# Routed experts in two parts of the tokens (six pairs of images and two), with the first part's expert blocks starting before the last pair is routed

## The reference

```python
x = x + conv_ref(group_norm(x))      # filters of 7x7 made per image from softmax keys, layer norm, relu;
                                     # then a depthwise 7x7 convolution with them
t = to_tokens(x)                     # (16, 256, 128)
t = t + attention(layer_norm(t))     # tanh features, softmax(q q^T / sqrt(128)) times the tokens, per image
# mixture of experts on layer_norm(t), 4096 tokens, 8 experts, hidden size 256, the best 2 of 8 per token:
scores = xf @ router_w + router_b
topk_p, topk_i = top_k(softmax(scores), 2)
h = xf @ w1[e] + b1[e]
gated = silu(h @ wg[e] + bg[e]) * (h @ wv[e] + bv[e])
y = gated @ w2[e] + b2[e]
t = t + sum over the 2 chosen experts of topk_p * y
```

## Time and profile before

| | |
|---|---|
| profiled execution, its own time | 386.41 us |
| its span, first to last instruction | 384.6 us |
| median of 3 runs | 386.43 us |
| busy share of the span | PE 79%, DVE 62%, POOL 43%, ACT 34% |
| first multiplication of a block | at 243.86 us |
| last scatter issued | at 360.52 us |
| granted TensorE clock, mean | 0.87 of full speed |

### The profile page before, as it was taken

The page is one execution under the profiler, slowest core; times in us unless marked ns, Lnnn a source line. Parts: engine busy times, 40 slices in busy tenths (PEclk is TensorE's granted clock), DMA queues, the critical chain, the costliest instruction groups (busy, mean ns, idle before and its releaser), DMA issues.

```text
span 384.6 us, 7449 instructions
## 1 busy us (share of the span) xinstructions
PE 302.8 (79%) x1731; PEld 239.7 (62%) x1732; DVE 236.7 (62%) x1006; ACT 132.4 (34%) x443; POOL 164.2 (43%) x187
## 2 busy tenths in 40 slices
PE   1686989998989899998876661599999999999200
PEld 1264667786868777777664440388878787888100
DVE  2433475488887877676866652266666676666164
ACT  0312221425152515141303012266656565666000
POOL 3000010030256565555455577046656566666400
PEclk9958896999999999989887655599999999999755
DMA  7722241221523000101010013223332322231197
GB/s 221 250 80 67 84 125 28 85 68 30 182 79 97 31 30 21 38 21 37 22 35 29 29 56 107 55 80 81 85 94 84 89 77 83 80 93 59 48 322 288
DMA packets 29945, 33.37 MB, mean 87 GB/s; under 512 B 5096, under 2 KB 23740, under 8 KB 29658
## 3 DMA queue, kind: packets, MB, share of 16 engines
q1 hardware_dynamic: 23312, 22.00, 18.9%
q0 software_dynamic: 4384, 8.60, 6.7%
q10 hardware_dynamic: 2218, 2.42, 1.8%
HBM read 21.76 MB, written 11.75 MB: 87 GB/s over the span
## 4 chain that ended last, share of the span: by engine, by line
PE 44%; issue 21%; POOL 21%; DMA 5%; DVE 4%; SPq 3%; ACT 1%; POOLq 0%; DVEq 0%; ACTq 0%
POOL rows_dram L410 15%; PE bank L1324 8%; PE bank L1312 5%; PE bank L1307 5%; PE bank L1308 5%; PE bank L1317 4%; PE bank L833 3%; DMA w_high<-moe_dram 2%; PE bank L876 2%; POOL ln_rstd L437 2%; PE bank L1302 2%; SPq L1160 2%; PE bank L978 2%; POOL ln_rstd L433 2%; PE bank L914 1%
## 5 line engine op out<-in xcount | busy, mean ns | idle before, releaser
L1132 POOL DMA_INDIRECT moe_dram<-ys,xs x72 | 70.4, 978 | 51.2 <-issue 30.8
L410 POOL DMA_INDIRECT rows_dram<-row,slot x64 | 62.7, 979 | 18.2 <-issue 18.2
L1324 PE MATMUL bank<-w_all,gatedt 128*128 x288 | 44.1, 276 | 0.2 <-ACT gatedt L1175 0.2
L1249 DVE SCALAR_TENSOR_TENSOR ys<-b_all,xs,bank 128x128 f32<-128x128 f32 x72 | 25.0, 347 | 28.5 <-issue 27.0
L1259 DVE SCALAR_TENSOR_TENSOR gated<-bank,xs,silu 128x256 f32<-128x256 f32 x72 | 34.8, 483 | 10.2 <-ACT silu L1183 7.8
L1183 ACT ACTIVATE silu<-bank 128x256 f32<-128x256 f32 x72 | 27.6, 383 | 35.7 <-PE bank L1312 35.7
L1324 PEld LDWEIGHTS bank<-w_all,gatedt 128*128 128x128 f32 x288 | 38.0, 192 | 0.4 <-issue 0.4
L1307 PE MATMUL bank<-w_high,x_high 128*128 x72 | 35.6, 494 | 0.0
L978 PE MATMUL bank<-zhat,const 121*128 121x256 f32 (+1 forms) x128 | 31.2, 399 | 0.0
L1312 PE MATMUL bank<-w_high,x_low 128*128 x72 | 30.3, 421 | 0.7 <-issue 0.7
L423 POOL TENSOR_TENSOR frstd<-fvar,minus_half 128x2 f32<-128x2 f32 x8 | 5.7, 708 | 57.5 <-DVE fvar L703 57.5
(11 more groups left out here) (172 smaller groups left out, 593.7 us busy)
## 6 DMA issues: line engine op xcount, KB each, us to landing
xs<-rows_dram SPq DMA_DIRECT2D x72, 66.0 KB, 1.8
xc<-in_x SPq DMA_DIRECT2D x8, 256.0 KB, 2.9
wgv<-in_wg SPq DMA_DIRECT2D x8, 256.0 KB, 2.9
wgv<-in_wv SPq DMA_DIRECT2D x8, 256.0 KB, 3.4
xt<-in_xt SPq DMA_DIRECT2D x4, 512.0 KB, 4.6
xt<-moe_dram SPq DMA_DIRECT2D x8, 256.0 KB, 6.0
w_high<-moe_dram SPq DMA_DIRECT2D x8, 256.0 KB, 6.6
out<-w_high ACTq DMA_DIRECT2D x8, 256.0 KB, 5.6
```

Source lines behind the costliest of these rows:

```text
L410: pool.indirect_dma_start(rows_dram, bass.IndirectOffsetOnAxis(ap=slot[:, f % 2, 2 * t + k:2 * t + k + 1], axis=0), row[:, f % 2, t, k, :] ...
L1132: pool.indirect_dma_start(moe_dram, bass.IndirectOffsetOnAxis(ap=xs[:, u, C + 1:C + 2].bitcast(U32), axis=0), ys[:, u, :], None, bounds_ch ...
L1324: last = pe.matmul(bank_y[v][:, 0:C], gatedt[:, v, h * P:(h + 1) * P], w2_all[:, bass.ds(e * (2 * C) + h * C, C)], start=(h == 0), stop=(h ...
```

## The change

The tokens are split in two parts: pairs 0 to 5 and pairs 6 and 7. Each part has its own `rows_dram`, `moe_dram`, running count, pads and table. What it does, by place:

- 78 blocks in place of 72: 55 for the first part (48 full ones and up to 7 more for partly filled ones) and 23 for the second. All are written out; there is no loop any more. The ring has 14 places.
- Experts' weights are made in rounds 1 to 8. There are 12 rounds (0 to 11). Stage E of pair 7 is cut in steps that stand between the blocks (`last_pair`: PE at steps 5, 8, 17 and 28, DVE at 2, 10 to 14, 16 to 22, 24 to 26 and 30, ACT at 6, 7 and 14).
- The table of the first part is computed at the end of round 10 and copied in round 11; its eight pads are all written by SP. The second part's table comes at DVE steps 24 to 30, its eight pads go between SP's loads of blocks 47 to 54.
- POOL sends the first tile's two rows of a pair in the round of its slots, the other six in the next round. Pair 7's eight sends go behind scatters 23, 26, 29 and 32, two each.
- SP loads the first part's results (12 tensors) between the loads of blocks 68 to 73, DVE adds them at steps 62 to 73, and SP stores them. Only pairs 6 and 7 are left for the end.
- In round 11 attention goes ahead of the ranks on PE. `bank_g` is one bank in place of two.

The diff, cut to its core:

```diff
-UNROLL = 12
-BLOCKS = -(-(2 * TOKENS // P + EXPERTS - 1) // UNROLL) * UNROLL
+SPLIT = 6
+HALVES = ((0, SPLIT), (SPLIT, PAIRS))
+COUNTS = tuple(2 * (end - begin) * PAIR_TOKENS // P + EXPERTS - 1 for begin, end in HALVES)
+BLOCKS = sum(COUNTS)
+RING = 14
...
-        rounds = PAIRS + STAGES - 1
+        rounds = PAIRS + STAGES - 3
+        LAST = PAIRS - 1
...
-        expert_rounds = [1, 2, 3, 4, 5, 6, PAIRS + 3, PAIRS + 4]
+        expert_rounds = list(range(1, EXPERTS + 1))
...
                     if f is not None:
-                        pool.wait_ge(row_done, f + 1)
-                        pool.wait_ge(row2_done, f + 1)
-                        dispatch(f, range(0, TILES // 2))
+                        dispatch(f, range(1, TILES // 2))
...
+                    if e is not None:
+
+                        pool.wait_ge(row_done, e + 1)
+                        pool.wait_ge(row2_done, e + 1)
+                        dispatch(e, range(0, 1))
...
-                experts["gpsimd"](pool)
+                dispatch(LAST - 1, range(1, TILES))
+
+                def last_dispatch(t):
+                    pool.wait_ge(row_done, PAIRS)
+                    pool.wait_ge(row2_done, PAIRS)
+                    dispatch(LAST, range(t, t + 1))
...
+                        if e == LAST - 1:
+                            experts["table"](dve, 0)
...
-                    if e == PAIRS - 1:
-
-                        experts["tables"](dve)
+                    if e == SPLIT - 1:
+
+                        experts["tables"](dve, 0)
...
+                    if d is not None and c is None:
+
+                        attention(i, d)
+                    if i == rounds - 1:
+                        experts["table_columns"](pe, 0)
...
+    def gpsimd(pool, last_dispatch):
+        for j in range(NB):
+            u = j % U
             pool.wait_ge(S["ys_done"], j + 1)
...
+            t, k = divmod(j - 23, 3)
+            if 0 <= t < TILES and k == 0:
+                last_dispatch(t)
...
+        write_pads(0, range(E))
+        for j in range(NB):
+            u = j % U
+            e = j - (A - E)
+            if 0 <= e < E:
+                write_pads(1, (e,))
+            if entry(j) == 0:
+                rows_ready(half_of(j))
+            if j >= U:
+                sp.wait_ge(ys_sent[u], 16 * (j // U))
+            row0 = sp.value_load(table[0:1, half_of(j), 0, entry(j):entry(j) + 1], min_val=0, max_val=ZERO)
+            sp.dma_start(xs[:, u, :], rows_dram[half_of(j)][bass.ds(row0, P), :]).then_inc(xs_loaded[u], 16)
+            p = j - (A + U - 1)
+            if p == 0:
+                all_sent(sp, A)
+            if 0 <= p < SPLIT:
+                load_result(sp, p, 0)
+                load_result(sp, p, 1)
+        for p in range(SPLIT):
+            store(sp, p)
+        all_sent(sp, NB)
+        for p in range(SPLIT, PAIRS):
+            load_result(sp, p, 0)
+        for p in range(SPLIT, PAIRS):
+            store(sp, p)
...
+            if j >= 2:
+                scale(j - 2)
+            last_pair(j)
+            p, k = divmod(j - (NB - 2 * SPLIT - 4), 2)
+            if 0 <= p < SPLIT:
+                if k == 0:
+                    first_sum(p)
+                else:
+                    second_sum(p)
```

More of the change, by code:

```diff
@@ L1005, in _ @@
                         last.then_inc(fraw_psum, 1)
-                    if d is not None:
-                        pe.wait_ge(e_done, 4 * (d + 1))
-                        after(pe, t1_done, through(i, CC))
-                        after(pe, t2_done, d)
-                        for h in range(CHUNKS):
-                            for s in range(2):
-                                for k in range(CHUNKS):
-                                    last = pe.matmul(bank_o[:, (h * 2 + s) * C:(h * 2 + s + 1) * C], e_attn[:, s, k, h * P:(h + 1) * P],
-                                                     z[:, d % 2, k * 2 + s, :], start=(k == 0), stop=(k == CHUNKS - 1))
-                        last.then_inc(attn_psum, 1)
+                    if d is not None and c is not None:
+                        attention(i, d)
                     if b is not None:
@@ L1030, in _, with last_pair @@
                         pe.wait_ge(bgt_done, 1)
-                experts["tensor"](pe)
+                def last_pair(j):
+                    if j == 5:
+                        router_input(rounds, LAST)
+                    if j == 8:
+                        router(rounds, LAST)
+                    if j == 17:
+                        ranks(rounds, LAST)
+                    if j == 28:
+                        experts["table_columns"](pe, 1)
+                experts["tensor"](pe, last_pair)
 def expert_programs(sb, sem, out, g):
@@ new lines, in gpsimd, with load_result, all_sent @@
+            if 0 <= t < TILES and k == 0:
+                last_dispatch(t)
+    def load_result(queue, p, k):
+        halves = moe_dram[p >= SPLIT].rearrange("(k n p t) c -> k n p (t c)", k=2, n=P, t=TILES)
+        into = y_second[p] if k else y_first[:, p, :, :]
+        queue.dma_start(into.rearrange("n t c -> n (t c)"), halves[k, :, p]).then_inc(y_loaded[p], 16)
+    def all_sent(queue, count):
+        for u in range(U):
+            queue.wait_ge(ys_sent[u], 16 * len(range(u, count, U)))
@@ new lines, in store, with write_pads, rows_ready @@
+    def store(queue, p):
+        queue.wait_ge(S["sum_done"], p + 1)
+        queue.dma_start(out[:, p], y_second[p]).then_inc(S["stored"], 16)
+    def sync(sp):
+        def write_pads(k, some):
+            sp.wait_ge(S["pad_at_ready"], k + 1)
+            sp.wait_ge(S["consts"], 2)
+            for e in some:
+                row0 = sp.value_load(pad_at[0:1, k, e:e + 1], min_val=0, max_val=ZERO)
+                sp.dma_start(rows_dram[k][bass.ds(row0, P), :], pad_row[:, :]).then_inc(S["pads_sent"], 16)
+        def rows_ready(k):
+            sp.wait_ge(S["table_ready"], k + 1)
+            sp.wait_ge(S["zeros_sent"], 16 * 2)
+            sp.wait_ge(S["pads_sent"], 16 * E * (k + 1))
+            for s in range(2):
+                sp.wait_ge(g["sent"][s], 16 * 2 * TILES * len(range(s, HALVES[k][1], 2)))
+        write_pads(0, range(E))
[23 more added lines that the diff above has]
+            store(sp, p)
@@ L1265, in vector, with first_sum @@
[L1265 to L1277 removed]
+        def first_sum(p):
             dve.wait_ge(y_loaded[p], 16 * 2)
```

547 lines of the change are left out of this document (305 added, 242 removed).

## The result

The changed kernel took 370.04 us (median of 4 runs, 367.73 to 377.3) beside 386.35 us for the kernel before (4 runs, 382.36 to 390.68): ratio 0.959, 95% interval 0.948 to 0.970. It is faster; 372 was predicted, within 360 to 380. The profiled execution took 369.19 us, its span is 367.4. Where a comparison rests on a single profiled execution I count from block 0's transpose, for the rounds run at different speeds from one execution to the next: attention of round 4 starts at 74.11 us here and at 79.90 in a second profile of the same kernel.

A forecast was written before the change was run, and what follows sets the result against it. PE and DVE bound the rounds, PE the blocks, DVE the end, with a hole before block 0. Block 0 at 220.7, scatter 77 at 358.5 with 15 added between blocks, plus 11.7: span 370.2, time 372 us, range 360 to 380.

The forecast's parts named there:

- Weights in rounds 7 and 8, +2.6: Making experts 6 and 7's weights in rounds 7 and 8 delays everything behind by 2.6 us, bounds 0.7 and 3.9.
- Block 0 at 220.7: At the seam, pads end last and release block 0's load; PE starts block 0 at 220.7 us, 23.2 earlier.
- Scatter 0 hidden by a microsecond: POOL has pair 6's rows ready at 228.7 us, about a microsecond before scatter 0 at 229.8.
- 78 blocks at 1.476, no gaps at turns: Scatter 77 comes 113.7 us after scatter 0 if nothing is added; the gaps at ends of turns go.
- Pair 7's steps, 4.5: Pair 7's stage E between the blocks adds 4.5 us, bounds 1.7 (PE alone) and 10 (all of PE and DVE).
- Pads and clock, 5 + 1: Part two's pads and POOL's sends stall blocks by 5 us (2 to 8); half clock afterwards adds 1 (0 to 3).
- Results, 2: Part one's results reach DVE's step 62 late if SP or POOL is late: 2 us added, 0 to 4.
- Twelve sums, 2.5: Twelve additions of 0.69 us between blocks exceed DVE's free 0.5 by 0.2 each: 2.5 added, 0 to 8.3.
- The end, 11.7: From the last scatter to the end, with only two pairs left: 11.7 us in place of 24.1.
- that the work hides (359): Rival, 20%: DVE's free time and the ring cover everything between blocks but PE's 1.7 us; 359, within 357 to 366.
- That the queues bound the blocks (382): Rival, 9%: SP's and POOL's queues bound from block 33 on, adding 25 us; 382, within 378 to 387.
- rival of half clock: Rival, 5%: PE's waits at blocks 33 to 73 lower the clock, 1.0 us per block; 27 blocks give 397.

The follow-up runs named there:

- run with the table ahead: Changed kernel with the first part's table transposes and copy moved ahead of attention (PE) and logits (DVE) in round 11; 376.05 us, ratio 0.981.
- written-out kernel before: Kernel before the change with its loops over turns written out, nothing else; 386.35 us, ratio 0.998.
- run that adds at the end: Changed kernel with part one's results loaded, added and stored at the end again, with those of part two; 380.92 us, ratio 0.988.
- version with pads and additions moved: Changed kernel with part two's pads written ahead in the rounds and the twelve additions three steps later; 363.67 us, ratio 0.945.
- all parts together: Changed kernel with pads ahead, additions three steps later, table ahead, and pair 7's exponential on POOL instead of ACT; 363.55 us in undisturbed turns, ratio 0.945.

## Why the prediction was right, step by step

The total was right to 2 us of the median, and the mechanism was the forecast's, but single terms were off by more, on both sides. Against the sum, in the profiled execution: block 0 came 4.4 early, scatter 0 came 1.0 later behind it than costed (10.1 in place of 9.1), the way to scatter 77 took 0.3 more, the end 0.2 more. That leaves the span 2.8 short of 370.2. Of the 4.4, 3.5 is luck of this execution: in the second profile of the same kernel round 4 came 2.3 later than before the change, not 3.5 earlier.

- **Weights in rounds 7 and 8, +2.6.** The two rounds grew by 2.4, as costed. From round 5's to round 10's attention the changed kernel took 99.72 against 99.01: only 0.7 more, since round 9 fell to its short form. That was this execution, not the change.
- **Block 0 at 220.7.** It came at 216.33. Of the 4.4, 3.5 had been gained before round 4 (74.11 against 77.59) by the start of this execution, 1.9 is the term above, and 1.0 was lost. About half of that is the pads: they came 1.22 us apart, not 1.12. The other half is the table: the pads did not end last, as the prediction had it, the table did, by half a microsecond. The prediction named that as a thing to watch ("if round 11 holds back the table"). The run with the table ahead gave that half microsecond back.
- **Scatter 0 hidden by a microsecond.** It was not: pair 6's last send ended at 226.16, 9.8 behind block 0's transpose in place of 8.0, and scatter 0 started 1.7 after its `ys` had ended. Nobody waits for it; POOL's lag is back at 0.77 by scatter 3.
- **78 blocks at 1.476, no gaps at turns.** Holds. The written-out kernel before shows by its trace that the gaps went with the turns.
- **Pair 7's steps, 4.5.** 6.3. The added part is ACT's two table loads: the prediction counted PE's and DVE's work and looked at no `Exp` between `Silu`. Without it 4.4 is left (6.3 - 1.9). The Trainium skill (ScalarE: Activation LUTs, the section on what a table load costs) gives 1283 ns for the load, as here, and a drain of 1380 ns with each change. The trace does not show the drain: the load starts 0.02 after the activation before it has ended, and the next activation 0.01 after the load.
- **Pads and clock, 5 + 1.** 6.3 + 0. SP took 2.45 per block (2.23 predicted) and POOL's lag at scatter 33 was 7.9 (6.5 to 8.5 predicted), 7.2 beyond the steady 0.77. The clock stayed at full: 1.00 between 295 and 312 us with PE busy for 14.05 of 17.00.
- **Results, 2.** 2.45, the term best hit in size. In the changed kernel it is SP that is late, as the prediction allowed: scatter 54 had landed 3.4 us before SP issued the load of block 68 (323.87), still catching up from the pads. What the prediction didn't say is that POOL is on time there only because the stall at the pads had let it catch up; where the stall was taken away, POOL was late and the wait was 2.9 or 4.3.
- **Twelve sums, 2.5.** 1.6. Both together are 4.06, by the run that adds at the end.
- **The end, 11.7.** 11.9 from the last scatter's issue.

The extras between blocks come to 16.9 against 15. The rivals: that the work hides (359) falls for the changed kernel, but the version with pads and additions moved is 4 to 5 us from it. That the queues bound the blocks (382) named the right queues with too large a price. In the rival of half clock 27 blocks at 1.0 make 398 rather than 397, and nothing hangs on it. That POOL stops beside additions falls by the row of the 78 scatters (durations min/median/max in ns). Eight of them overlap one of the twelve additions in time and took 977 or 978 ns:

```profile
L1245 POOL DMA_INDIRECT moe_dram<-ys,xs x78: 977/979/999, 226.5 to 355.5; - x78
```

That doesn't refute the rule of the Trainium skill (SBUF — State Buffer, the section on two separate sides). The section speaks of a DVE operation in a two-port mode, and of one with two inputs in SBUF only against a POOL operation that reads SBUF; the additions are of the second kind, and the prediction applied the first to them. What the runs show is that this addition did not hold up these scatters.

Half clock in the blocks is refuted by the windows: 1.00 from 226.4 to 356.5.

## What to carry to other kernels

When work is moved under a pipeline whose bound is another engine, add up what each in-order queue gets extra and how fast it can catch up (here 10.2 us of sends against 0.2 per block). The lag outlives the place it was made at, and comes out at the next thing that waits for it, even 20 blocks on. Until then it eats what the ring has in hand, so that a single slow transfer shows. A stall that such a lag causes also lets the lag go, so removing the stall alone gives only part of it; the next wait has to be moved as well. Before a step is moved to another engine, look for that operation's price on that engine: on ACT the exponential took 0.23 us and the two changes of function around it 2.56; on POOL the power in its place took 5.47.

## What the runs showed of the hardware that I had not expected

- The first rounds come out with different clocks from one execution to the next. Granted clock from 40 to 75 us, with round 4's attention at 74.11 (changed kernel, first profile), at 79.90 (again), and at 85.16 (pads and additions, some of whose pads are also written in these rounds):

```profile
40.00:75.00 35.00, 32.04 (x161) 24.11 (x161) 21.68 (x85) 10.99 (x41) 3.93 (x5) 0.97 0.29 84
```

```profile
40.00:75.00 35.00, 32.04 (x129) 22.50 (x129) 18.25 (x70) 10.00 (x39) 3.23 (x4) 0.82 0.21 62
```

```profile
40.00:75.00 35.00, 32.59 (x112) 22.39 (x111) 16.45 (x62) 6.44 (x23) 2.97 (x4) 0.66 0.37 99
```

  In all three PE is busy 32.0 to 32.6 of 35, with 161, 129 and 112 matmuls done. Between the two profiles of the same kernel round 4 moved by 5.8 us; round 10 gave 1.7 back, and the times are 3.4 apart (369.19 and 372.59). So a change of 1% can't be read from a few medians of this kernel; distances within one trace can.
- A power on POOL took 5.47 us for 128 x 32, where 128 x 4 takes 1.04 to 1.22: (5.47 - 1.04)/28 = 0.16 us for each further column.
- In one set of turns every kernel took 8 to 12% longer, with idle time on PE, DVE and ACT that the trace puts down to nothing in the program.
- Most block loads land 1.8 to 1.9 us after their issue, but single ones take 3 to 5.3 (block 51 with pads and additions moved, 3.18; block 70 with all parts together, 5.30).
